# Softmax attention of a four-block kernel: 64-row score pairs, one shared ring of two PSUM banks, and the last power in groups

## The chip, the core and the metric

The kernel runs on one NeuronCore of a Trainium2 chip. Five engines work side by side and wait for each other through semaphores: TensorE (PE, matmul; its weight loads are PEld), VectorE (DVE), ScalarE (ACT), GpSimd (POOL) and SyncE (SP, which issues most DMAs). Matmuls write PSUM, which has eight banks of 512 fp32 columns on 128 partitions. The metric is the device time of one execution in microseconds; lower is better.

## The reference, cut to what matters

The reference is a chain of four blocks on x of shape (2, 1024, 256): a differential softmax attention, a routed block with attention and an FFN, an attention over a memory with an entmax, and an FFN with ternary weights. Each is added to x after a layer norm. Only the first block (and the start of the next stage) is touched:

```
qkv = layernorm(x) @ Wqkv             # q1, k1, q2, k2: 16 heads of 8; v: 16 heads of 16
A1 = causal_softmax_attention(q1, k1, v)      # scores q.k / sqrt(8)
A2 = causal_softmax_attention(q2, k2, v)
diff = A1 - lam * A2
diff = diff / sqrt(mean(diff^2) + 1e-5) * (1 - LAMBDA_INIT)     # per head and token
x = x + layernorm(diff @ Wproj)
```

## The kernel before, in words

`attention_inputs` (0 to 65 us) normalizes x, multiplies by Wqkv and splits each query and key into three bf16 parts (high, middle, low); the parts go to DRAM (`qk_parts`). SyncE loads them back for each head as stacks of rows: six parts of eight dimensions, 48 rows, for each of the two attentions j. The product of a query stack and a key stack gives the score with nearly fp32 precision. In `QS` and `KS` before the change rows 0 to 47 hold the stack, rows 48 to 95 are zero and rows 96 to 98 hold the row maximum in three bf16 parts (`QS`) against a constant near one (`KS`); j is a dimension of the tile. GpSimd fills the constant rows with three memsets (L198, L203, L208), and the load of head 0 (L161) waits for the last.

`attention_heads` runs 16 heads. For each head and each of the four (j, batch) pairs there are two sets of score matmuls:

- the natural set (`unit_scores`, L642): queries on the partitions, keys on the columns, 96 rows of contraction. Units of at most 512 columns, 40 per head, with the causal mask added on the diagonal by a matmul of an identity and a mask (L645). They go to three PSUM banks `nat`; VectorE reduces each to a row maximum (L515). The maxima of a head are joined (L519), turned by TensorE into the bank `misc` (L653), split in three bf16 parts by VectorE from that bank (L530 to L538), and written by six DMAs into rows 96 to 98 of `QS` (L420).
- the transposed set (`scores`, L678): keys on the partitions, queries on the columns, 128 rows of contraction, so that the maximum is subtracted by the matmul itself. A head has nine chunks n with four matmul groups c = (j, batch) each. Each group goes to one of two banks `sc`, and ScalarE takes the exponential (L610). GpSimd zeroes the part above the diagonal of five chunks (L482). Two chunks later TensorE multiplies the four probability tiles by the values (`values`, L698, four matmuls on 32 columns of the array each), accumulating in `OT`.

The order of TensorE is written out by hand in `period` (L717 on): for each chunk n and each c, the scores of c; then the natural units that are due (of the next head and of the one after it, spread evenly over the 36 places); after c = 1 the turned outputs of the last head (in chunks 2 and 3) and the values of chunk n - 2. The outputs of a head are copied from `OT` by ScalarE (L592, at the end of chunk 1), turned in two rounds by TensorE into `misc` (L714), copied again by ScalarE (L599), normalized by VectorE (L544, L546), and combined and squared by GpSimd (L450, L455, L460). GpSimd also runs a slice of the ternary weights of the last block in each head (L340 to L351, after the diagonal of chunk 4), and raises the mean square of the outputs to the power -0.5 for each head (L468, 16 columns). The last head's power (604.42 to 607.35 us) is the last instruction of the stage; `output_and_route` starts after it with VectorE's scaling of the outputs (L937).

## Time and profile before

| | us |
|---|---|
| median of 3 runs (1664.35 to 1668.11) | 1667.57 |
| the profiled execution | 1665.8 |
| its span, first to last instruction | 1664.0 |
| TensorE busy / weight loads | 1490.1 / 1010.6 |
| VectorE busy | 1249.8 |
| ScalarE busy | 1109.4 |
| GpSimd busy | 1080.9 |
| granted TensorE clock, mean over the span | 0.963 |

Busy shares are averages over stages with different limits. The attention heads span 65 to 608 us. In a timeline row the first number is the start in us from the beginning of the span, the second the time to the end of the merged group; `xN` counts the merged instructions (a fp32 matmul is two records), and brackets hold the idle time of the engine before the group and what ended it.

### The profile page before, as it was taken

Reading aid. Unit: us, or ns where it says so; the run is one execution under the profiler, and the core shown is the slowest. Engines: PE = TensorE matmul, PEld = TensorE weight load, DVE = VectorE, ACT = ScalarE, POOL = GpSimd, SP = SyncE. Lnnn points to the kernel's source line nnn. Section 1 sums busy time; section 2 is a strip of 40 time slices with the busy share of each in tenths; the row PEclk is TensorE's granted clock in tenths of the full one; section 3 lists DMA queues with packets and bytes.
Section 4 is the critical chain, followed back from the end, with each engine's and each line's share of the span. In section 5 each row is a group of like instructions: output and inputs, shape, how many; then the busy total and the mean of one; then the engine's idle time right before and its main releaser. Section 6 shows DMA issues by size and latency. Waiting matters only on the chain. (4 is left out here: it accounts for less than half of the span.)

```text
span 1664.0 us, 26578 instructions
## 1 busy us (share of the span) xinstructions
PE 1490.1 (90%) x8478; PEld 1010.6 (61%) x8540; DVE 1249.8 (75%) x3420; ACT 1109.4 (67%) x2385; POOL 1080.9 (65%) x1273
## 2 busy tenths in 40 slices
PE   7899999999999857887848999999999999987998
PEld 4334434434434236766646888878888888776675
DVE  5688788788788229652359999999999999973433
ACT  2146666666666737222237999999999999994332
POOL 6205466566566572142248999999999999973353
PEclk9779999999999979999979999999999999999999
DMA  5301001001000033830000000000000100000000
GB/s 203 114 21 38 23 22 38 22 22 39 21 22 21 2 103 116 320 121 17 35 1 1 1 1 1 1 1 1 1 1 1 51 1 1 1 1 1 1 26 26
DMA packets 39812, 59.84 MB, mean 36 GB/s; under 512 B 9132, under 2 KB 33592, under 8 KB 38776
## 3 DMA queue, kind: packets, MB, share of 16 engines
q1 hardware_dynamic: 39528, 56.03, 10.4%
q10 hardware_dynamic: 144, 2.10, 0.3%
q8 instruction: 69, 1.13, 0.3%
q14 instruction: 71, 0.58, 0.1%
HBM read 40.93 MB, written 16.78 MB: 35 GB/s over the span
## 5 line engine op out<-in xcount | busy, mean ns | idle before, releaser
L610 ACT ACTIVATE a_PT<-a_sc 128x512 f32<-128x512 f32 x576 | 317.7, 600 | 187.8 <-PE a_sc L678 128.7
L515 DVE TENSOR_REDUCE a_mpart<-a_nat 128x1 f32<-128x512 f32 (+3 forms) x640 | 364.1, 627 | 78.5 <-PE a_nat L645 41.4
L2046 DVE BATCH_NORM_STATS2 c_stat<-c_R 128x6 f32<-128x512 f32 x576 | 380.9, 678 | 1.7 <-ACT c_R L1965 1.6
L2010 POOL TENSOR_SCALAR c_R<-big,c_negtau 128x256 f32<-128x256 f32 x264 | 300.6, 1165 | 33.1 <-DVE c_negtau L2079 27.0
L2010 POOL TENSOR_SCALAR c_R<-c_Z,c_negtau 128x256 f32<-128x256 f32 x255 | 290.7, 1164 | 16.0 <-DVE c_negtau L2112 15.2
L642 PE MATMUL a_nat<-mem 96*128 96x512 bf16 (+3 forms) x768 | 242.7, 343 | 22.0 <-DVE a_mpart L515 11.8
L1882 PE MATMUL c_z<-mem,c_R 128*128 128x256 f32 x1024 | 231.5, 379 | 0.0
L482 POOL TENSOR_SCALAR_AFFINE_SELECT a_PT<-a_PT 128x512 f32<-128x512 f32 x128 | 79.0, 636 | 221.9 <-ACT a_PT L610 221.9
L1965 ACT ACTIVATE c_R<-c_Z,c_negtau 128x256 f32<-128x256 f32 x513 | 215.8, 516 | 0.4 <-DVE c_negtau L2112 0.4
L1965 ACT ACTIVATE c_R<-big,c_negtau 128x256 f32<-128x256 f32 x504 | 212.6, 515 | 3.2 <-DVE c_negtau L2079 1.7
L1882 PEld LDWEIGHTS c_z<-mem,c_R 128*128 128x128 f32 x1024 | 192.9, 190 | 25.4
L678 PE MATMUL a_sc<-mem 128*128 128x512 bf16 (+3 forms) x706 | 196.8, 326 | 9.0 <-ACT a_PT L610 6.2
L678 PEld LDWEIGHTS a_sc<-mem 128*128 128x128 bf16 x768 | 61.2, 97 | 179.4 <-ACT a_PT L610 148.4
L698 PE MATMUL a_OT<-a_PT,a_VH 128*32 128x512 f32 (+3 forms) x1536 | 154.6, 498 | 3.3 <-POOL a_PT L482 3.2
L1894 PE MATMUL c_T<-ident,c_R 128*128 128x128 f32 x768 | 106.7, 282 | 35.9 <-ACT c_R L1960 35.3
L1882 PE MATMUL c_z<-mem,c_hT 128*128 128x256 f32 x512 | 119.6, 388 | 8.8 <-ACT c_hT L1989 8.8
L642 PEld LDWEIGHTS a_nat<-mem 96*128 96x128 bf16 x768 | 76.2, 99 | 76.4 <-DVE a_mpart L515 48.3
L1906 PE MATMUL c_y<-mem,c_R 128*128 128x256 f32 x512 | 120.7, 386 | 0.0
L1894 PEld LDWEIGHTS c_T<-ident,c_R 128*128 128x128 f32 x768 | 85.9, 142 | 56.7 <-ACT c_R L1960 46.7
L1960 ACT ACTIVATE c_R<-c_T 128x512 f32<-128x512 f32 x192 | 104.0, 595 | 22.5 <-PE c_T L1894 22.5
L1882 PEld LDWEIGHTS c_z<-mem,c_hT 128*128 128x128 f32 x512 | 98.7, 195 | 24.4 <-ACT c_hT L1989 9.4
L645 PE MATMUL a_nat<-mask,ident_bf 128*128 128x128 bf16 x512 | 106.7, 227 | 0.0
(313 smaller groups left out, 2445.1 us busy)
## 6 DMA issues: line engine op xcount, KB each, us to landing
mem<-qk_parts SPq DMA_DIRECT2D x360, 32.0 KB
qk_parts<-a_parts SPq DMA_DIRECT2D x16, 384.0 KB, 2.6
made<-f_made SPq DMA_DIRECT2D x24, 256.0 KB, 2.8
mem<-made SPq DMA_DIRECT2D x3, 2048.0 KB, 7.7
X<-in_L_attn_x_dram SPq DMA_DIRECT2D x4, 512.0 KB, 6.9
mem<-in_L_ffn_wq_dram SPq DMA_DIRECT2D x1, 2048.0 KB, 13.9
ternary<-f_W_T ACTq DMA_DIRECT2D x1, 2048.0 KB, 8.7
mem<-in_L_ffn_wo_dram SPq DMA_DIRECT2D x1, 2048.0 KB, 14.4
```

The costliest lines, as they stand in the source:

```text
L515: dve.tensor_reduce(mpart[:, b, j:j + cnt, i, k0 // 512], src, AX.X, ALU.max).then_inc(s_max, 1)
L610: act.activation(PT[:, n % 3, c, :], sc[:, u % 2, :], ACT.Exp, scale=SCALE0).then_inc(s_exp, 1)
L642: ins = pe.matmul(out, QS[0:MROW, h.buf, j, q:q + P], KS[0:MROW, h.buf, j, b * T + k0:b * T + k0 + w], start=True, stop=diag >= w)
L645: ins = pe.matmul(out[:, diag:diag + P], K.ident_bf[:], K.mask[:], start=False, stop=True)
L678: ins = pe.matmul(sc[:, u % 2, col:col + w], KS[:, h.buf, j, b * T + kt * P:b * T + (kt + 1) * P], QS[:, h.buf, j, b * T + q0:b * T + q0 + ...
L698: ins = pe.matmul(OT[32 * c:32 * c + 32, q0:q0 + w], VH[:, h.buf, b * TB + kt, :], PT[:, n % 3, c, col:col + w], start=(kt == 0), stop=(kt ...
L1882: ins = pe.matmul(z_ps[:, n % SCORE_BANKS, e * NMEM:(e + 1) * NMEM], L, G[:, m, h, :], start=(m == 0), stop=(m == 1))
L1894: ins = pe.transpose(T_ps[:, n % TURN_BANKS, (2 * e + m) * P:(2 * e + m + 1) * P], whole(i, h)[:, m * P:(m + 1) * P], K.ident[:])
L1906: ins = pe.matmul(y_ps[:, k % 2, 0:D], weights(i, h, m), K.VO[:, m, h, :], start=(n == 0), stop=(n == 15))
L1965: act.activation(split(i, h) if r < NR else whole(i, h), scores_of(i)[:, h, :], ACT.Relu, bias=threshold(i, r, h)).then_inc(s_ra[r], 1)
L2010: pool.tensor_scalar(split(i, h) if r < NR else whole(i, h), scores_of(i)[:, h, :], threshold(i, r, h), 0.0, ALU.add, ALU.max).then_inc(s_ ...
L2046: dve.bn_stats(stat[:, r, b, :], R[:, slot(i), b, :]).then_inc(s_stat, 1)
```

## The change

- `QS` and `KS` lose their dimension j: attention j = 0 has rows 0 to 50, j = 1 rows 64 to 114 (48 of the stack, 3 of the maximum). Both score sets now contract over 48 or 51 rows in one half of the array, and natural units go in pairs (j = 1, j = 0), into four banks. The two zero memsets go; one memset of a tile half as wide stays.
- The mask of 128 rows is added in two steps of 64 rows, on the half that the unit uses; a copy of identity and mask with swapped halves is made by four DMAs.
- The bank `misc` goes. The turned maxima and the two turned outputs take their turn in the two banks of the exponentials, in one written-out order (`IN_TURN`); each waits for whoever read the bank two places before. ScalarE copies the turned maxima to SBUF (`mcopy`), and VectorE splits from there.
- The order in `period`: scores of c = 0 (or 2), the natural pairs that are due (20 pairs over 18 places), scores of c + 1, then as before turned outputs and values. The turn of the maxima has a fixed place, after the first score of chunk 6. The scores of a chunk go in the order j = 0, 1, 0, 1. ScalarE copies a turned output after the exponential of c = 1 instead of after c = 3.
- The power of the last head goes to the next stage, in four groups of four columns; `scaled(g)` waits for its own group. There GpSimd's constants (iota, memsets, selects) move behind the first root and the memory's root.

```
-STK = 6 * HD0
-MROW = 96
+STK, SIDE = 6 * HD0, 64
 def max_units():
+    shapes = [[(i, 0, 512)] for i in range(3, TB)] + [[(7, 512, 512)], [(2, 0, 384)], [(6, 512, 384)],
+                                                      [(1, 0, 256), (5, 512, 256)], [(0, 0, 128), (4, 512, 128)]]
+    return [(j, segs) for segs in shapes for j in (1, 0)]
+SET_ORDER = (0, 2, 1, 3)
+MAX_CHUNK = 6
+def turned_banks():
+    order = [("max", 0)]
+    for h in range(H0):
+        for n in range(len(PROB_CHUNKS)):
+            for c in range(4):
+                order.append(("exp", h, n, c))
+                if n == MAX_CHUNK and c == 0 and h + 1 < H0:
+                    order.append(("max", h + 1))
+                if n in (2, 3) and c == 1 and h > 0:
+                    order.append(("out", h - 1, n - 2))
+    return order + [("out", H0 - 1, r) for r in range(2)]
...
             root(0)
             pool.wait_ge(s_xn, GT)
-            pool.memset(K.QS[:].bitcast(F32), 0.0).then_inc(s_zero, 1)
+            pool.memset(K.KS[:].bitcast(F32), BF16_ONES).then_inc(s_zero, 1)
...
-            pool.memset(K.KS[0:MROW].bitcast(F32), 0.0).then_inc(s_zero, 1)
...
-            pool.memset(K.KS[MROW:P].bitcast(F32), BF16_ONES).then_inc(s_zero, 1)
...
-        nat, sc, OT, misc = ps("nat", [P, 3, 512]), ps("sc", [P, 2, 512]), ps("OT", [P, T]), ps("misc", [P, 512])
+        nat, sc, OT = ps("nat", [P, 4, 512]), ps("sc", [P, 2, 512]), ps("OT", [P, T])
+        bank_of = lambda *what: sc[:, TURN_OF[what] % 2, :]
...
+            def copy_max(h):
+                act.wait_ge(s_mT, h.count(1, 1))
+                if h.n > 0:
+                    act.wait_ge(s_msp, h.count(1))
+                act.activation(mcopy[:], bank_of("max", h.n)[0:32, 0:P], ACT.Copy).then_inc(s_mc, 1)
...
+            def unit_pair(h, u):
...
+                if NU * h.n + u >= 4:
                     pe.wait_ge(s_max, h.count(NU, u - 2))
+                pair = [units[u], units[u + 1]]
+                for n in range(len(pair[0][2])):
+                    for e, (b, j, segs) in enumerate(pair):
+                        (i, k0, w), rows = segs[n], slice(SIDE * j, SIDE * j + STK)
+                        q, out = b * T + i * P, nat[:, (u + e) % 4, n * w:(n + 1) * w]
+                        ins = pe.matmul(out, QS[rows, h.buf, q:q + P], KS[rows, h.buf, b * T + k0:b * T + k0 + w],
+                                        start=True, stop=i * P - k0 >= w)
...
+                    for half, (unit, mask) in enumerate(((K.ident_bf, K.mask), (K.ident_swap, K.mask_swap))):
+                        for e, (b, j, segs) in enumerate(pair):
+                            (i, k0, w), side = segs[n], slice(SIDE * j, SIDE * j + SIDE)
+                            diag = i * P - k0
+                            if diag < w:
+                                out = nat[:, (u + e) % 4, n * w + diag:n * w + diag + P]
+                                ins = pe.matmul(out, unit[side, :], mask[side, :], start=False, stop=half == 1)
...
+            def bank_for(*what):
+                k = TURN_OF[what]
+                if k >= 2:
+                    kind, h, *rest = IN_TURN[k - 2]
+                    if kind == "exp":
+                        pe.wait_ge(s_exp, 4 * NCH * h + 4 * rest[0] + rest[1] + 1)
+                    elif kind == "max":
+                        pe.wait_ge(s_mc, h + 1)
+                    else:
+                        pe.wait_ge(s_ons, 2 * h + rest[0] + 1)
+                return bank_of(*what)
...
-                    for c in range(4):
+                    for c in (0, 2):
                         scores(h, n, c)
-                        k = 4 * n + c
-                        for _ in range(NU * (k + 1) // (4 * NCH) - NU * k // (4 * NCH)):
+                        if n == MAX_CHUNK and c == 0 and h.next(1).exists():
+                            turn_max(h.next(1))
+                        k = 2 * n + c // 2
+                        for _ in range(NU // 2 * (k + 1) // (2 * NCH) - NU // 2 * k // (2 * NCH)):
                             next(between, None)
-                        if c == 1:
+                        scores(h, n, c + 1)
+                        if c == 0:
                             if last.exists() and VLAG <= n < VLAG + 2:
                                 turn_outputs(last, n - VLAG)
...
+            for g in range(NG):
+                last = K.rms[:, rows(g), H0 - 1]
+                pool.tensor_tensor(last, last, K.mhalf[:, 0:GT], ALU.pow).then_inc(s_rms, 1)
             ternary_slice(pool, K, H0 - 1, s_tern, 0)
+            y_root(0)
...
             def scaled(g):
+                dve.wait_ge(s_rms, g + 1)
```

## Rows read from the trace of the kernel before

**Rows 1.** Windows by stage: busy time and instructions per engine, TensorE clock, DMA share, GB/s.
```profile
65.00:98.00 33.00, 30.46 (x104) 9.45 (x105) 31.63 (x61) 0.00 (x0) 1.17 (x2) 0.55 0.16 43
...
128.75:563.18 434.43, 416.71 (x3177) 172.67 (x3231) 349.72 (x699) 302.34 (x561) 265.28 (x433) 1.00 0.10 26
```
**Rows 2.** Timeline of TensorE, one middle head: start, length, instructions (PV, L698).
```profile
284.33 1.07 PE L698 MATMUL a_OT<-a_PT,a_VH 128*32 128x512 f32 x8
287.44 1.07 PE L698 MATMUL a_OT<-a_PT,a_VH 128*32 128x384 f32 x16
...
291.51 1.06 PE L698 MATMUL a_OT<-a_PT,a_VH 128*32 128x512 f32 x8
...
295.15 1.06 PE L698 MATMUL a_OT<-a_PT,a_VH 128*32 128x512 f32 x8
...
301.69 1.07 PE L698 MATMUL a_OT<-a_PT,a_VH 128*32 128x512 f32 x8
...
315.45 1.07 PE L698 MATMUL a_OT<-a_PT,a_VH 128*32 128x512 f32 x8
```
**Rows 3.** Timeline of one slot of the last head, TensorE and ScalarE.
```profile
582.44 1.07 PE L698 MATMUL a_OT<-a_PT,a_VH 128*32 128x256 f32 x16
...
583.44 0.60 PE L678 MATMUL a_sc<-mem 128*128 128x512 bf16 x2
...
583.87 1.08 ACT L610 ACTIVATE a_PT<-a_sc 128x512 f32<-128x512 f32 x2 [0.67 <-PE a_sc L678]
...
584.52 0.88 PE L678 MATMUL a_sc<-mem 128*128 128x512 bf16 x2 [0.47 <-ACT a_PT L610]
...
585.33 1.06 PE L698 MATMUL a_OT<-a_PT,a_VH 128*32 128x512 f32 x8
```
**Rows 4.** Timeline of ScalarE in slot 2 of the middle head.
```profile
289.84 1.03 ACT L592 ACTIVATE a_OTS<-a_OT 128x1024 f32<-128x1024 f32 x1
290.74 1.11 ACT L610 ACTIVATE a_PT<-a_sc 128x512 f32<-128x512 f32 x2
```
**Rows 5.** Timeline of GpSimd: diagonal selects of chunks 4 and 7.
```profile
301.15 1.22 POOL L482 TENSOR_SCALAR_AFFINE_SELECT a_PT<-a_PT 128x512 f32<-128x512 f32 x2 [5.83 <-ACT a_PT L610]
...
313.74 0.64 POOL L482 TENSOR_SCALAR_AFFINE_SELECT a_PT<-a_PT 128x512 f32<-128x512 f32 x1
```
**Rows 6.** Timeline of VectorE and SP after the split, and DMA landing (KB, us).
```profile
305.99 3.99 DVE L515 TENSOR_REDUCE a_mpart<-a_nat 128x1 f32<-128x512 f32 x7
306.09 3.68 SPq L420 DMA_DIRECT2D mem<-a_msplit  x6
...
mem<-a_msplit SPq DMA_DIRECT2D x6, 4.0 KB, 1.7
```
**Rows 7.** Timeline of the routed stage: matmuls of 64 rows on alternating halves.
```profile
729.41 1.14 PE L1547 MATMUL b_s<-b_qkT 64*128 64x256 f32 x8
730.48 0.29 PE L1549 MATMUL b_s<-mask,ident_bf 128*128 128x128 bf16 x2
```
**Rows 8.** Window of the last head.
```profile
555.00:590.00 35.00, 26.54 (x179) 7.48 (x180) 1.51 (x5) 26.20 (x50) 23.91 (x39) 1.00 0.01 1
```
**Rows 9.** Timeline of the inputs: GpSimd's third memset, SP's issues, VectorE's last part.
```profile
40.56 5.21 POOL L208 MEMSET mem<- 32x6144 f32 x1 [1.48 <-DVE a_xn L230]
...
45.88 8.11 SPq L114 DMA_DIRECT2D mem<-qk_parts  x24
54.03 7.34 SPq L156 DMA_DIRECT2D qk_parts<-a_parts  x8
...
57.73 0.69 DVE L242 TENSOR_TENSOR a_parts<-a_rest,a_parts 128x512 bf16<-128x512 f32 x1 [0.51 <-POOL a_parts L194]
```
**Rows 10.** Timeline of GpSimd at the end of the heads and in the next stage.
```profile
604.42 2.93 POOL L468 TENSOR_TENSOR rms<-rms,mhalf 128x16 f32<-128x16 f32 x1 [0.75 <-DVE rms L554]
...
621.20 0.24 POOL L892 TENSOR_SCALAR f_yr<-f_ymv 128x4 f32<-128x4 f32 x1 [2.02 <-DVE f_ymv L946]
621.51 1.05 POOL L894 TENSOR_TENSOR f_yr<-f_yr,mhalf 128x4 f32<-128x4 f32 x1
```

More of the change, by code:

```diff
@@ L136, in attention_inputs @@
         (s_w, s_lam, s_ident, s_pool, s_pad, s_zero, s_st, s_mv, s_var, s_rstd, s_dve, s_xn, s_turned, s_xT, s_qk, s_v, s_hi, s_rest,
-         s_mid, s_lo, s_vc, s_lame) = (sem(n) for n in "w lam ident pool pad zero st mv var rstd dve xn turned xT qk v hi rest "
-                                       "mid lo vc lame".split())
+         s_mid, s_lo, s_vc, s_lame, s_swap) = (sem(n) for n in "w lam ident pool pad zero st mv var rstd dve xn turned xT qk v hi rest "
+                                       "mid lo vc lame swap".split())
         block = ctx.enter_context(nc.Block())
@@ L152, in _ @@
             load_ffn(sp, K, K.w_ffn)
+            sp.wait_ge(s_ident, 3)
+            for whole, swapped in ((K.ident_bf, K.ident_swap), (K.mask, K.mask_swap)):
+                for half in range(2):
+                    sp.dma_start(swapped[SIDE * half:SIDE * half + SIDE, :],
+                                 whole[SIDE * (1 - half):SIDE * (2 - half), :]).then_inc(s_swap, 16)
             for g in range(NG):
@@ L359, in attention_heads @@
     qk_parts, VA = K.qk_parts, K.VA
-    units = [(b, n) + u for b in range(2) for n, u in enumerate(max_units())]
+    units = [(b,) + u for b in range(2) for u in max_units()]
     NU, NCH = len(units), len(PROB_CHUNKS)
@@ L616, in period @@
                             copy_sums(last)
-                        if VLAG <= n < VLAG + 2:
-                            copy_turned(last, n - VLAG)
+            copy_max(Head(0, 0))
             heads(act, period)
@@ L659, in maxima @@
                     return
-                for u in range(FIRST, NU):
-                    unit_scores(first, u)
+                for u in range(FIRST, NU, 2):
+                    unit_pair(first, u)
                     yield
-                for u in range(FIRST):
-                    if u == GAP or not second.exists():
-                        turn_max(first)
-                        if not second.exists():
-                            return
-                    unit_scores(second, u)
-                    yield
+                if second.exists():
+                    for u in range(0, FIRST, 2):
+                        unit_pair(second, u)
+                        yield
             def scores(h, n, c):
                 u = 4 * n + c
-                j, b = c // 2, c % 2
-                if not isinstance(h.n, int) or 4 * NCH * h.n + u > 1:
-                    pe.wait_ge(s_exp, h.count(4 * NCH, u - 1))
-                col = 0
+                j, b = SET_ORDER[c] // 2, SET_ORDER[c] % 2
+                rows = slice(SIDE * j, SIDE * j + STK + 3)
+                bank, col = bank_for("exp", h.n, n, c), 0
                 for kt, q0, w in PROB_CHUNKS[n]:
-                    ins = pe.matmul(sc[:, u % 2, col:col + w], KS[:, h.buf, j, b * T + kt * P:b * T + (kt + 1) * P],
-                                    QS[:, h.buf, j, b * T + q0:b * T + q0 + w], start=True, stop=True)
+                    ins = pe.matmul(bank[:, col:col + w], KS[rows, h.buf, b * T + kt * P:b * T + (kt + 1) * P],
+                                    QS[rows, h.buf, b * T + q0:b * T + q0 + w], start=True, stop=True)
                     col += w
@@ L736, in period @@
                     pass
-            for u in range(FIRST):
-                unit_scores(Head(0, 0), u)
-            for _ in maxima(Head(0, -1)):
-                pass
+            for u in range(0, FIRST, 2):
+                unit_pair(Head(0, 0), u)
+            for k, _ in enumerate(maxima(Head(0, -1))):
+                if k == (NU - FIRST + GAP) // 2 - 1:
+                    turn_max(Head(0, 0))
             heads(pe, period)
```

101 lines of the change are left out of this document (42 added, 59 removed).

## The prediction, made before the change was run

> **What bounds the kernel now.** The windows by stage come first: the sixteen heads of the first attention (65 to 608 us) are a third of the span, and TensorE reads 96% busy through them [rows 1]. That looks like a TensorE bound. The timeline says otherwise. The starts of the probability-value products ("PV", L698), one per chunk, mark slots; nine slots are a head, 284.33 to 315.45, so 31.1 us [rows 2]; heads 1 to 14 together take 434.43, 31.0 each [rows 1]. Now the last head, which has no score sets for maxima ("natural" units) left to do. Its slot is still 585.33 - 582.44 = 2.89 us [rows 3], and it is a chain of latencies, not of work: PV 1.00, its next score matmul to its exponential 0.43 (583.44 to 583.87), two exponentials to the release of a bank and the last score before the next PV, 1.46. An undisturbed slot of a middle head is 3.11 (287.44 - 284.33) [rows 2]: the natural matmul between the second score and PV adds its 0.22, plus a mask. So most of the natural matmuls' time is hidden already, and halving them cannot return 7 us per head.
>
> **The change, part by part, for a middle head.** I count from one PV start (0). Score c=2 starts at 1.00, its exponential at 1.43, the next at 1.91 (two take 1.08, the latency of one being 0.60) [rows 3]; score c=0 of the next slot waits for the first, 2.07; c=1 for the second, 2.56; PV at 2.89.
>
> *Pairs in halves.* Natural matmuls leave the place before PV and stand between scores c=0/c=1 and c=2/c=3. The gaps are 0.49 and 0.55 us. Does a pair fit? In the routed stage 64-row matmuls on alternating halves are in the trace: eight records, four fp32 products of 256 columns, 1024 cycles each, 4096 cycles or 1.71 us in a row; the masks after them start at 730.48, 1.07 us after the first [rows 7]. The halves overlap; about 0.2 of the 1.07 is entry and exit. So a 512-column pair beside a score takes one extra 0.22, masks (four of 128 columns instead of two) 0.11 to 0.22, and it fits: slot 2.9 instead of 3.1. Bounds: full cover 2.89; nothing gained by masks, 3.05.
> The Trainium skill, TensorEngine Tiling (Array Packing), Key Properties, says that changing the tiling mode drains TensorE; the 0.2 us above agrees. By rows I charge 0.1 for each extra switch, around the two turns of outputs. (By the page alone that term would only be unknown, not absent.)
>
> *Turned outputs in the exponentials' ring.* Slot 2 today is 4.07 (287.44 to 291.51) [rows 2]: the ScalarE copy of the sums starts at 2.40 and holds the first exponential to 3.30 (289.84, 290.74) [rows 4]; the turn needs only the copy. New: the turn takes a bank and waits for that first exponential, 3.30 + 0.65 = 3.95, then 0.58 of turning: PV at 4.53, with the switch 4.55. Slot 3: turn after exponential 0, 3.8 against 3.64. The copies of turned outputs fall in the PV hole, free.
>
> *Turned maxima.* They too take a ring place: score c=1 of slot 6 waits for its own slot's exponential: 3.13 instead of 2.56, slot 3.46 where an undisturbed one today is 3.1. The small ScalarE copy sits in the same hole. What follows: VectorE's split, six DMAs (3.68 issuing, 1.7 to landing) [rows 6] and the wait at the next head. The split ends about 4.7 after PV of slot 5 (VectorE does two reductions first), the rows land near 10.1; the next head's first score is at 11.6. No wait, about 1.5 us spare (0 to 2). SP's 24 loads for a later head go out first and are 8 us long at a head's start, as for head 0 (45.88 to 54.0) [rows 9].
>
> *Four natural banks against VectorE.* Seven reductions take 3.99, so 0.57 each, 1.15 a pair [rows 6]; VectorE is 80% busy [rows 1], so it does not bound on average. But the schedule emits twenty pairs over eighteen gaps, and in slot 4's first gap two: the second waits for the pair emitted 1.0 us earlier. That one is ready at 1.7 and reduced at 2.95; score c=1 goes at 3.4 instead of 2.56. Slot 4: 3.7, so slots 4 and 5 together 6.6, against 6.54 (295.15 to 301.69) [rows 2]. (Bounds for slot 4: 2.9 and 3.9.) After the split slot 7 loses about 0.3.
>
> *GpSimd, next in line.* From the diagonal selects of chunk 4 (301.15) through one ternary slice and the outputs to the end of select 7 (313.74 + 0.64) is 13.2 us [rows 5]; PV of slot 0 waits for that. Nothing of it changes. The selects start 0.33 before PV of slot 5, so PV of slot 5 to PV of slot 0 cannot be under 12.9; today it is 13.76 (301.69 to 315.45) [rows 2]. TensorE's own way is 3.46 + 3 x 2.89 + 0.3 to 0.8 = 12.4 to 12.9. I take 13.0.
>
> Head: 2.9 + 4.55 + 3.8 + 3.7 + 2.9 + 13.0 = 30.85, against 31.1: -0.25. Bounds: every gap covered and no GpSimd limit 2.89 x 6 + 4.5 + 3.7 + 3.46 = 29.0; the upper ends 31.9.
>
> **Sum.**
> Inputs: two of three 5.2 us memsets go. SP waited for the last (40.56 to 45.8) before loading head 0, and its last parts left at 54.03 + 7.34 = 61.4. VectorE's last part is ready at 57.73 + 0.69 = 58.4, and one issue is about 0.9; new end 59.4: -2.0 [rows 9]. Four swap copies use SP while it waits: 0 (up to +0.5).
> Start of heads: VectorE paces it (31.6 busy of 33) [rows 1]; one bank more lets TensorE leave earlier, -0.6 (0 to -1.2). Head 0, no outputs or slices: nine slots at about -0.22, -2.0 (0 to -3).
> Heads 1 to 13: 13 x -0.25 = -3.3. Head 14 has no second set, today 434.43 - 13 x 31.12 = 29.9; new 30.85, +0.9. Head 15: slots 2 and 3 alone, +0.6.
> End: the second turn no longer waits for the first copy, -0.7. Power: the 16-column one (2.93) stood between stages; the first group of four costs 1.05 (as L894), TensorE waits for that only: 2.93 - 1.05 = -1.9 [rows 10]. The other three run beside VectorE's scaling; ternary slice and y root come 4.2 later in the stage, of which the root waited 2.0 for its input [rows 10], and the fill of constants (about 1.3) moves behind it: within 0.9.
> Total -2.0 - 0.6 - 2.0 - 3.3 + 0.9 + 0.6 - 0.7 - 1.9 = -9.0. The profiled execution took 1665.8 (span 1664.0 and 1.8 around it): 1656.8; it lies 1.8 under the median of the runs, so 1658 in that frame.
>
> **Rivals.**
> *A, the chain is looser than I count* (GpSimd and VectorE catch up, the double pair hides). For it: the slack of 0.5 in each gap. Against: slots 2 and 3 are long today with and without natural units. Head 29.0 to 30.2: -2.0 x 13 and -0.9 for head 14 and the rest give 1632 at the full end. Chance 0.17.
> *B, TensorE's work is the bound after all*, as its 96% suggest. Scores and natural sets are 36 x 0.22 us each per head, so half of both is 7.9; VectorE's 25 us (349.72 / 14) then bounds, -6 a head: about 1570. The last head's 2.89 speaks against it. Chance 0.03. The same page, Theoretical Speedup, gives up to 2x for contractions of 64 or less; by that rule alone this would be the result.
> *C, bank waits cost a little more*: masks at 0.055 each in five gaps and 0.3 more at the double pair; head 31.5, 13 x 0.4 = +5.2, head 14 +1.5, the rest -6: 1668. Chance 0.19.
> *D, slower: the granted clock.* Natural units alone ran at a mean of 0.55 in the first stretch [rows 1]; the last head kept 1.00 with TensorE 76% busy [rows 8]. With half the rows quiet TensorE could fall to 1.2 GHz between 130 and 560. At that level PV and two scores on the chain, 1.44, double; with a third of the slots low this is 9 x 0.48 = 4.3 a head, +60: 1720. It decides once more than a twentieth of the slots are low. Chance 0.07.
> *E, the halves do not overlap for bf16 into separate banks.* A pair then needs 0.66 to 0.88 in a gap of 0.49 to 0.55, about 0.3 a gap; outside the GpSimd stretch that is 2.5 a head, +35: 1693. Rows 7 speak against it. Chance 0.04.
>
> **Numbers.** Forecast 0.50, A 0.17, B 0.03, C 0.19, D 0.07, E 0.04. Range: 1640 to 1672 leaves out B, D, E and the far half of A on one side. The likeliest case alone holds 1651 to 1664. A measurement of this kernel can tell about 0.2% (3.3 us) from none. Faster: A, B and nine tenths of the forecast, 0.66; same: the rest of the forecast and half of C, 0.14; slower: half of C, D, E, 0.20.
>
> **What would show it.** Slots of the new profile: 2.9 undisturbed, 4.5 and 3.8 where outputs turn, about 3.5 with turned maxima, 3.7 in slot 4 behind two pairs. ScalarE idle of about 0.5 before c=2. Select of chunk 7 ending right before PV of slot 0. Granted clock 1.00 from 105 to 590. Heads starting near 63, VectorE's first scaling about 1.9 earlier after the outputs. Wrong would be a head under 30 (then the ring or GpSimd does not bind) or over 31.5, or a score waiting for the rows of the maxima.

## The result, and the profile after

The changed kernel takes 1674.87 us (median of 6 runs, 1671.64 to 1680.71); the kernel before, run beside it, 1667.24 (1663.92 to 1669.40). The ratio is 1.0053, 95% interval 1.0038 to 1.0067: slower by about half a per cent, where 1658 was forecast. The profiled execution is the slowest of the six (1680.71, span 1679.0), so the sums over its trace below come out larger than the difference of the medians. Medians and ranges are over all executions of a kernel, but ratios leave out an execution more than 1.5% above the kernel's fastest, which concerns scores48 alone (two of its four).

The loss shows first in one column of one view, the granted clock. Windows of TensorE in the changed kernel: busy time and instructions, granted clock (1.00 is 2.4 GHz, 0.50 is 1.2), DMA share, GB/s.
```profile
100.00:110.00 10.00, 9.70 (x49) 0.50 0.04 13
110.00:120.00 10.00, 8.85 (x94) 0.83 0.01 2
200.00:260.00 60.00, 49.65 (x520) 1.00 0.09 26
260.00:270.00 10.00, 8.82 (x62) 0.66 0.06 15
570.00:580.00 10.00, 7.74 (x42) 0.50 0.00 0
```
Before, the clock was 1.00 in all of heads 1 to 14 [rows 1] and in the last head [rows 8]. Now it comes up late at the start of head 0, dips in some of the middle heads, and has a mean of 0.55 from the first to the last slot of the last head (569.29 to 604.80).

The schedule itself came out as forecast. The starts of the probability-value products (PV) of head 1, all at clock 1.00, answer to [rows 2]. Timeline of TensorE:
```profile
128.27 1.06 PE L741 MATMUL a_OT<-a_PT,a_VH 128*32 128x512 f32 x8
131.15 1.07 PE L741 MATMUL a_OT<-a_PT,a_VH 128*32 128x384 f32 x16
...
135.21 0.63 PE L753 MATMUL a_sc<-ident,a_OTS 128*128 128x128 f32 x4 [1.11 <-ACT a_PT L635]
...
135.77 1.06 PE L741 MATMUL a_OT<-a_PT,a_VH 128*32 128x512 f32 x8
139.57 1.06 PE L741 MATMUL a_OT<-a_PT,a_VH 128*32 128x512 f32 x8
143.22 1.07 PE L741 MATMUL a_OT<-a_PT,a_VH 128*32 128x384 f32 x16
146.11 1.06 PE L741 MATMUL a_OT<-a_PT,a_VH 128*32 128x512 f32 x8
...
159.24 1.06 PE L741 MATMUL a_OT<-a_PT,a_VH 128*32 128x512 f32 x8
```
The differences, with the three starts that are left out here (149.63, 152.64, 155.52), are 2.88, 4.62, 3.80, 3.65, 2.89, 3.52, 3.01, 2.88, 3.72: the forecast had 2.9, 4.55, 3.8, 3.7, 2.9 and 13.0 for the last four (13.13 here). The head is 30.97, forecast 30.85. The wait of 1.11 ahead of the turned outputs is the ring's: TensorE stands until the exponential has left the bank.

In the last head the same work takes longer. Timeline of TensorE in the changed kernel, PV of slots 0, 6, 7 and 8, slot 7 to be read against [rows 3]:
```profile
569.29 1.93 PE L741 MATMUL a_OT<-a_PT,a_VH 128*32 128x512 f32 x8
...
596.44 1.93 PE L741 MATMUL a_OT<-a_PT,a_VH 128*32 128x256 f32 x16
...
599.60 1.09 PE L721 MATMUL a_sc<-mem 51*128 51x512 bf16 x2 [0.68 <-ACT a_PT L635]
600.62 1.93 PE L741 MATMUL a_OT<-a_PT,a_VH 128*32 128x512 f32 x8
604.80 1.93 PE L741 MATMUL a_OT<-a_PT,a_VH 128*32 128x512 f32 x8
```
and PV of slots 0 and 8 in the kernel before:
```profile
563.18 1.07 PE L698 MATMUL a_OT<-a_PT,a_VH 128*32 128x512 f32 x8 [0.66 <-POOL a_PT L482]
...
588.22 1.06 PE L698 MATMUL a_OT<-a_PT,a_VH 128*32 128x512 f32 x8
```
PV is 1.93 long instead of 1.06, and the slot 600.62 - 596.44 = 4.18 instead of 2.89. There is no more work in it than before; it is the latency chain at half the clock. From PV of slot 0 to PV of slot 8 the last head takes 35.5 us (569.29 to 604.80) instead of 25.0 (563.18 to 588.22).

Start and tail, in the order first exponential, copy of the last sums, power by groups, scaling. Timeline of ScalarE, GpSimd and VectorE in the changed kernel:
```profile
95.27 0.60 ACT L635 ACTIVATE a_PT<-a_sc 128x512 f32<-128x512 f32 x1 [9.10 <-PE a_sc L721]
610.87 1.02 ACT L611 ACTIVATE a_OTS<-a_OT 128x1024 f32<-128x1024 f32 x1 [2.48 <-PE a_OT L741]
619.03 2.01 POOL L950 TENSOR_TENSOR rms<-rms,mhalf 128x4 f32<-128x4 f32 x2 [0.98 <-POOLq L379]
620.08 0.76 DVE L985 TENSOR_TENSOR f_dn<-DIFF,rms 128x256 f32<-128x256 f32 x2 [1.37 <-POOL rms L950]
```
and of the kernel before (its power is in [rows 10]):
```profile
98.81 0.60 ACT L610 ACTIVATE a_PT<-a_sc 128x512 f32<-128x512 f32 x1 [39.52 <-remote]
595.51 1.02 ACT L592 ACTIVATE a_OTS<-a_OT 128x1024 f32<-128x1024 f32 x1 [4.78 <-PE a_OT L698]
607.72 2.77 DVE L937 TENSOR_TENSOR f_dn<-DIFF,rms 128x256 f32<-128x256 f32 x8 [3.37 <-PEq L364]
```

From these the balance of the profiled executions up to the scaling (620.08 against 607.72, +12.36): at the first exponential the changed kernel is 3.5 ahead; at slot 0 of head 1 only 0.5 (128.27 against 128.75), so head 0 gave back 3.0 while the clock stayed low; heads 1 to 14 take 569.29 - 128.27 = 441.0 against 434.4 (+6.6), where fourteen undisturbed heads would be 433.6; the last head from PV of slot 0 to PV of slot 8 takes 35.5 against 25.0 (+10.5); from there to the copy of the sums 6.1 against 7.3 (-1.2), and from the copy to the scaling 9.2 against 12.2 (-3.0). The head 0 of this execution is an unlucky one: in three kernels below with the same start (last_full, last_half, moved) the clock came up earlier, and from the first exponential to slot 0 of head 1 they took 30.0, 31.5 and 31.2 where this execution took 33.0 and the kernel before 29.9. The remaining 2.6 of the span fall in later stages, which the change doesn't touch except for GpSimd's order, and are within what two single executions of this kernel differ by.

### The profile page after: what moved, and what is told of

It is laid out like the page before. It is cut to its first block and busy times, and to the rows that moved or that the text cites. A ratio compares the mean times of both kernels' runs of the same rounds, so it can differ in the third digit from the quotient of the medians.

```text
span 1679.0 us, 27707 instructions
## 1 busy us (share of the span) xinstructions
PE 1441.4 (86%) x9052; PEld 982.3 (59%) x9052; DVE 1249.7 (74%) x3420; ACT 1120.9 (67%) x2401; POOL 1070.8 (64%) x1274
## 5 line engine op out<-in xcount | busy, mean ns | idle before, releaser
L721 PE MATMUL a_sc<-mem 51*128 51x512 bf16 (+3 forms) x768 | 217.1, 349 | 53.8 <-ACT a_PT L635 51.7
L500 POOL TENSOR_SCALAR_AFFINE_SELECT a_PT<-a_PT 128x512 f32<-128x512 f32 x128 | 78.6, 638 | 242.1 <-ACT a_PT L635 241.9
L670 PE MATMUL a_nat<-mem 48*128 48x512 bf16 (+3 forms) x768 | 181.3, 353 | 23.6 <-DVE a_mpart L534 20.7
L721 PEld LDWEIGHTS a_sc<-mem 51*128 51x128 bf16 x768 | 55.2, 95 | 222.7 <-ACT a_PT L635 163.6
L741 PE MATMUL a_OT<-a_PT,a_VH 128*32 128x512 f32 (+3 forms) x1536 | 168.4, 536 | 2.9 <-POOL a_PT L500 1.7
L1954 PEld LDWEIGHTS c_y<-mem,c_R 128*128 128x128 f32 x512 | 98.4, 198 | 12.8
L1972 PE MATMUL c_T<-mem,ident 128*128 128x256 f32 x368 | 86.9, 379 | 0.0
```

The costliest lines, as they stand in the source:

```text
L670: ins = pe.matmul(out, QS[rows, h.buf, q:q + P], KS[rows, h.buf, b * T + k0:b * T + k0 + w], start=True, stop=i * P - k0 >= w)
L721: ins = pe.matmul(bank[:, col:col + w], KS[rows, h.buf, b * T + kt * P:b * T + (kt + 1) * P], QS[rows, h.buf, b * T + q0:b * T + q0 + w], ...
L741: ins = pe.matmul(OT[32 * c:32 * c + 32, q0:q0 + w], VH[:, h.buf, b * TB + kt, :], PT[:, n % 3, c, col:col + w], start=(kt == 0), stop=(kt ...
L1954: ins = pe.matmul(y_ps[:, k % 2, 0:D], weights(i, h, m), K.VO[:, m, h, :], start=(n == 0), stop=(n == 15))
```

## The experiments

The theory that was tested, **R (rows)**: a product that contracts over 48 or 51 rows leaves most of TensorE's array idle, and for this the chip grants the low clock, whatever the busy column says. The rivals: **I (idle stretches)**, the clock falls because the ring's waits leave TensorE idle; **S (schedule)**, the last head and the double pair are slow in themselves. Each kernel was timed against the kernel before on the same chip; ratios are to it, and where a kernel is set against the changed one, its 1.0053 is the other term.

### Rows in the kernel before: nat48 and short

nat48:
```
- QS[0:MROW, ...], KS[0:MROW, ...]   # natural products, 96 rows
+ QS[0:STK, ...],  KS[0:STK, ...]    # 48 rows
```


> The kernel before, its natural score products alone contracting over rows 0:48 instead of 0:96 (rows 48 to 95 were zero, so nothing is left out). Theory R (rows): TensorE's granted clock falls because instructions that contract over few rows leave most of the array idle. The last head has no natural products, so its first eight slots stay at 25.0 us and clock 1.00; the middle heads may show a first dip or none: 1667 to 1672 us. Theory I (idle gaps): the clock falls because the changed kernel's waits on the two-bank ring leave TensorE idle longer at a stretch; here no wait changes, so 1667 within 1 us and no dip. Both allow no change; a dip would speak for R alone.

short, with the line above and:
```
- MROW = 96
+ MROW = STK
- matmul(sc..., KS[:, ...], QS[:, ...])                      # turned score products, 128 rows
+ matmul(sc..., KS[0:STK + 3, ...], QS[0:STK + 3, ...])      # 51 rows
```
(GpSimd's second memset also fills rows 0 to 95 of `KS` with the constant now, since the maxima stand in rows 48 to 50.)


> The kernel before with every score product over few rows: maxima in rows 48:51, natural products over 48 rows instead of 96, turned score products over 51 instead of 128; banks, order, waits and all else as before. Theory R: the last head falls to the low clock and its slots 0 to 8 take about 31 us instead of 25.0, the middle heads show a few dips of 2 to 3 us, the start of head 0 comes up about 3 us later: +10 to +17 us, 1677 to 1684 us. Theory I (idle gaps from the ring): nothing changes, 1667 within 1 us, granted clock 1.00 in all of the last head.

Measured: nat48 1773.07 (1771.34 to 1779.95), ratio 1.0650 (1.0629 to 1.0671). short 2024.85 (2015.88 to 2035.94), ratio 1.2163 (1.2128 to 1.2198). Both theories missed nat48 by a hundred microseconds, and no theory foresaw the size of short. There are two different costs. Window of TensorE in nat48:
```profile
120.00:550.00 430.00, 421.72 (x2562) 0.98 0.08 22
```
and in short:
```profile
120.00:550.00 430.00, 429.76 (x1805) 0.57 0.06 15
```
In its middle heads nat48 is slow at full clock, so that loss is not the clock's. Timeline of TensorE in nat48, the rhythm of turned and natural products (weight loads left out):
```profile
320.15 0.39 PE L678 MATMUL a_sc<-mem 128*128 128x512 bf16 x1
...
320.48 0.39 PE L642 MATMUL a_nat<-mem 48*128 48x512 bf16 x1
...
320.79 0.39 PE L678 MATMUL a_sc<-mem 128*128 128x256 bf16 x2
```
and in the kernel before:
```profile
296.15 0.39 PE L678 MATMUL a_sc<-mem 128*128 128x512 bf16 x1
...
296.38 0.38 PE L642 MATMUL a_nat<-mem 96*128 96x512 bf16 x1
```
Before, the next product starts 0.23 us after the last (296.15, 296.38). Each change between a 48-row and a full product makes that 0.31 to 0.33: about 0.1 per change. A head of nat48 is 37.7 (PV starts 301.06 to 338.79) against 31.1; at 0.1 each that would be some 65 changes a head that nothing hides, an estimate. Over heads 1 to 14 of the profiled execution this comes to 89.2 (523.6 against 434.4). Another 26.3 lie ahead of head 1, and there the clock has its part: it stays at 0.50 from 70 to 140 us, where the kernel before has 1.00 from about 102 on, though nothing but the rows of the natural products differs. The last head, which has no natural products, takes the same 25.0 as before, at 1.00. The busy column gives no warning: the stalls count as busy (421.72 of 430).

short has fewer such changes than nat48 (its turned and natural products are of one mode and follow each other at 0.23 us), and yet the clock is 0.57 as a mean over heads in which TensorE reads 99.9% busy. No wait, bank or order was changed against the kernel before. That is theory R, and waits on a ring (theory I) cannot explain it, for there is no ring. Stalls at changes of rows hide in the busy column too, but nat48 has more of them and kept 1.00 from 150 us on.

### The last head: last_full and last_half
```
+ if not h.next(1).exists():
+     pe.wait_ge(s_max, NU * H0)
+     for _ in range(2):
+         pe.matmul(nat[:, k % 4, :], K.ident_bf[0:P, :], KS[0:P, h.buf, 0:512], start=True, stop=True)
```
at each of the last head's eighteen places; last_half has `0:STK` in place of `0:P`. The results are not used.

> The changed kernel with two idle products of 128x128 by 512 columns over all 128 rows (results unused) at each of the 18 places of the last head where the other heads have a pair of natural products. Theory R: the last head returns to clock 1.00 and slots of about 2.9 us, so slots 0 to 8 take about 25.5 instead of 31.3 us: -5 to -7 us against the changed kernel, 1668 to 1670 us (ratio to before 1.000 to 1.002). Theory I: the gaps are filled, so the same -5 to -7. Theory S (the last head is slow for the ring's own order, not for the clock): the added products only cost, 1675 or more.

> The same kernel as last_full, but the idle products contract over 48 rows only: the same number of instructions, columns and busy time. Theory R: the clock stays at the low level in the last head, slots 0 to 8 take 31 us or more: 1675 to 1677 us. Theory I (busy time or gaps decide, not rows): as last_full, 1668 to 1670 us. Theory S: 1675 or more.

Measured: last_full 1671.31 (1665.99 to 1674.80), ratio 1.0028 (1.0016 to 1.0039); last_half 1674.37 (1671.96 to 1680.34), ratio 1.0053 (1.0034 to 1.0072). Full rows gave back 0.0025 of 1666, 4.2 us where 5 to 7 were expected, half rows nothing. (The expectations count 31 us for slots 0 to 8 of the last head of the changed kernel; that is one slot short, and against the 25.0 of the kernel before stand 35.5.) Windows of TensorE in last_full:
```profile
560.00:570.00 10.00, 8.21 (x37) 0.58 0.01 2
570.00:580.00 10.00, 8.59 (x54) 0.91 0.01 2
```
and in last_half:
```profile
560.00:570.00 10.00, 8.54 (x36) 0.50 0.01 2
570.00:580.00 10.00, 9.11 (x45) 0.50 0.00 0
580.00:590.00 10.00, 9.03 (x65) 0.88 0.01 2
```
In these two executions the clock was already down when head 15 began (568.25 and 569.28): the last natural product of head 14 starts at 553.1 and 553.4, and PV takes 1.9 from 562.99 and 560.48 on. With full rows the clock is up again some 10 us earlier. This speaks for R over I, but weakly: last_half also came back in the end, and slots 0 to 8 took 30.1 in last_full and 30.2 in last_half, since the full-row products cost time of their own (slots of 3.25 at clock 1.00 where last_half has 2.88). S is out, since with 2.88 a slot at clock 1.00 is as short as before.

### The double pair: moved
```
- for _ in range(NU // 2 * (k + 1) // (2 * NCH) - NU // 2 * k // (2 * NCH)):   # two pairs at k = 8 and 17
+ for _ in range(1 + (k in (9, 17))):
```
(The expectation's "place 9 of 18" is k = 9, the second gap of slot 4.)

> The changed kernel with its double pair of natural products moved from after score product 8.0 to after 8.2's neighbour (place 9 of 18, the second of slot 4) and nothing else changed. The forecast's step for slot 4 (3.7, two pairs against VectorE's four maxima): there the double pair stands ahead of the pair of exponentials that the next product waits for; after the move slot 4 should take 3.1 to 3.3 us instead of 3.65, 13 or 14 times: -5 to -7 us, about 1668 to 1670. If slot 4 is bound elsewhere (VectorE's backlog moves along), slot 5 takes what slot 4 gives and the time stays at 1675. Theory R says nothing of it: the dips and the last head stay.

Measured: 1675.09 (1672.70 to 1676.80), ratio 1.0054 (1.0041 to 1.0067), the changed kernel's own. Timeline of TensorE in a head of moved, PV of slots 3 to 6 (that of slot 7 starts at 213.92):
```profile
200.83 1.07 PE L741 MATMUL a_OT<-a_PT,a_VH 128*32 128x512 f32 x8
203.71 1.07 PE L741 MATMUL a_OT<-a_PT,a_VH 128*32 128x384 f32 x16
207.11 1.07 PE L741 MATMUL a_OT<-a_PT,a_VH 128*32 128x512 f32 x8
210.78 1.07 PE L741 MATMUL a_OT<-a_PT,a_VH 128*32 128x256 f32 x16
```
Slot 4 fell to 2.88, and slots 5 and 6 took 3.40 and 3.67 for it: the 13.09 from PV 3 to PV 7 were 13.07. The expected second outcome: VectorE's backlog moved along, and from PV 5 to the next head's PV 0 it is 13.1 in the changed kernel and 13.2 in moved, the GpSimd limit of the forecast: PV of slot 0 waits for GpSimd's select (L500) in the head shown above.

### Filling the waits: warm, warm_all, warm_half, warm_one, warm_last
```
+ def fill_next(h, pairs, n):        # ahead of turn_outputs: n = 4 in slot 2, 1 in slot 3; heads 0 to 13 only
+     unit = NU * (h.n + 1) + FIRST + 2 * pairs
+     pe.wait_ge(s_max, unit - 2)
+     fill(nat[:, unit % 4, :], h.next(1).buf, n)    # the product of last_full, n times
...
+ elif h.n >= H0 - 2:                # a place with no pair left
+     pe.wait_ge(s_max, NU * H0 - 2)
+     fill(nat[:, 0, :], h.buf, 2)
...
+ fill(OT[:, 0:512], 0, 1)           # after each pair ahead of head 0
```
warm has all three over 128 rows; warm_all adds one more product at the end of every slot but slot 3; warm_half is warm with 48 rows (64 to 111) in each of these products; warm_one has none ahead of head 0 and one instead of two in the empty places; warm_last is warm_one without `fill_next`.

> The changed kernel with idle full-row products (128 rows, 512 columns, results unused) where TensorE otherwise waits: one after each pair ahead of head 0, four ahead of the turned outputs of slot 2, one ahead of those of slot 3, two at each place of heads 14 and 15 that has no pair. Theory R: the clock rises as early as in the kernel before (about 101 us), no dips in heads 1 to 13, and at most one short stretch of low clock in the last head: -10 to -15 us against the changed kernel, 1660 to 1665, the sum that the forecast made at full clock. If the dips come from something else (an event that lies outside the chain), the middle heads keep them and only the start and the last head gain: 1667 to 1670.

> As warm, and one more idle full-row product at the end of each slot but slot 3, where TensorE waits 0.34 to 0.47 us for the exponentials. Theory R: the dips are gone even where warm keeps one; the added product costs nothing where it fits (0.22 us in a gap of 0.34) and up to 0.1 us a slot where it does not: 1658 to 1672. If warm already has no dip, this is equal or up to 10 us worse.

> The kernel warm with every idle product contracting over 48 rows (64 to 111) instead of 128: the same instructions, columns and places. Theory R: the rows are what keeps the clock up, so most of warm's gain over the changed kernel is gone: dips in the middle heads, a low last head, 1671 to 1677. Theory I (idle stretches bring the clock down, whatever fills them): as warm, 1661 to 1665.

> The kernel warm with no idle products ahead of head 0 (in warm the first exponential came 0.8 us later for them) and one instead of two at each place of heads 14 and 15 without a pair (in warm nine slots of the last heads took 3.25 us instead of 2.88). If the clock stays: -0.4 to -1 us at the start, -2.5 to -3 at the end, 1659 to 1660, a version faster than both kernels. If one product in a place is too few: the last head falls to the low clock, 1664 to 1668.

> The kernel warm_one without the idle products ahead of the turned outputs: only heads 14 and 15 have any. Theory R: the last head stays up, the middle heads show their two to four dips of 2 to 3 us again: warm_one + 4 to + 9 us, 1664 to 1668.

| kernel | median (range) us | ratio to before (95%) |
|---|---|---|
| warm | 1662.67 (1661.55 to 1667.84) | 0.9988 (0.9980 to 0.9997) |
| warm_all | 1672.46 (1670.71 to 1677.59) | 1.0049 (1.0034 to 1.0063) |
| warm_half | 1659.69 (1657.55 to 1662.18) | 0.9968 (0.9956 to 0.9979) |
| warm_one | 1659.54 (1658.16 to 1663.87) | 0.9970 (0.9959 to 0.9982) |
| warm_last | 1666.28 (1664.18 to 1670.66) | 1.0002 (0.9993 to 1.0011) |

The work of the kernel is unchanged in all five; only products nobody uses were added, and three of them beat the kernel before, warm by as little as a measurement can tell. Window of TensorE over the middle heads in warm_one:
```profile
120.00:550.00 430.00, 371.00 (x3763) 1.00 0.09 26
```
warm_half has 370.04 busy and 1.00 there, the changed kernel 356.41 and 0.98, warm_last 357.41 and 0.97. The idle products ahead of head 0 did not help: in warm they had the clock at 0.84 over 70 to 80, but it was at 0.50 again from 100 until about 109.

warm_last less warm_one prices the dips of the middle heads at 6.7 us by the medians (1666.28, 1659.54), 5.3 by the ratios; the changed kernel less warm_last prices the last two heads at 8.5 (1.0053, 1.0002 of 1666). warm_all kept the clock and lost for its cost: nine slots of a head take 3.25, 4.62, 3.80, 3.64, 2.89, 3.53, 3.32, 2.88 and 3.82, together 31.75 instead of 30.97, since the product at a slot's end stands in the way of the next slot's turned products in three places.

warm_half is the miss of theory R as it was put: 48-row products cured the dips as well as full ones, and they cost less. From PV of slot 0 to PV of slot 8 its last head takes 26.1 at clock 1.00, that of warm 28.9, with slots of 2.89 and 3.25. So R alone is not the whole: few rows and idle time add up, and either is a lever. Rows did it without idle in short; idle products of few rows undid it in warm_half.

### The ring, the tail: ring and tail

ring is the kernel before with the change's `bank_for`, `copy_max` and `turned_banks`; `misc` is gone, three natural banks and all rows stay:
```
- nat, sc, OT, misc = ps("nat", [P, 3, 512]), ps("sc", [P, 2, 512]), ps("OT", [P, T]), ps("misc", [P, 512])
+ nat, sc, OT = ps("nat", [P, 3, 512]), ps("sc", [P, 2, 512]), ps("OT", [P, T])
...
- pe.transpose(misc[:, k * P:(k + 1) * P], OTS...)
+ pe.transpose(bank[:, k * P:(k + 1) * P], OTS...)     # bank = bank_for("out", h.n, r)
```


> The kernel before with the bank ring alone: turned maxima and turned outputs go through the two banks of the exponentials (as in the changed kernel, with the copy of the maxima on ScalarE), everything else as before, all contractions over 96 and 128 rows. The forecast's steps: slot 2 takes about 1.3 us more, slot 3 0.7 more, slot 6 0.3 more, with VectorE's work as before: +1 to +2 us a head, 1680 to 1700. Theory R: the clock stays at 1.00 in every head, since no product lost rows. Theory I: the waits on the ring bring dips and a low last head here too.

Measured: 1683.37 (1682.35 to 1685.83), ratio 1.0112 (1.0099 to 1.0125). Timeline of TensorE in a head of ring:
```profile
325.86 1.07 PE L737 MATMUL a_OT<-a_PT,a_VH 128*32 128x384 f32 x16
329.93 0.63 PE L749 MATMUL a_sc<-ident,a_OTS 128*128 128x128 f32 x4 [0.66 <-ACT a_PT L640]
330.48 1.07 PE L737 MATMUL a_OT<-a_PT,a_VH 128*32 128x512 f32 x8
```
Slot 2 is 4.62 against 4.07 (+0.55, forecast +0.48), slot 3 3.80 against 3.64, slot 6 344.57 - 340.82 = 3.75 against 3.16; the head 32.24 against 31.12, +1.1. The expectation's sizes were too large for slots 2 and 3 and too small for slot 6; its range for the whole held. The clock was 1.00 over 120 to 550: in the middle heads, where natural products fill the gaps, the ring's waits do not bring it down when the products have their rows. In the last head they do, once. Window, and timeline of TensorE in slot 2 of the last head of ring:
```profile
550.00:600.00 50.00, 41.51 (x292) 0.97 0.01 1
586.12 1.05 PE L749 MATMUL a_sc<-ident,a_OTS 128*128 128x128 f32 x4 [1.10 <-ACT a_PT L640]
587.11 1.94 PE L737 MATMUL a_OT<-a_PT,a_VH 128*32 128x512 f32 x8
```
TensorE waits 1.10 for the ring (it is busy 0.79 of the 2 us from 584 to 586), the clock reads 0.54 over 586 to 588, and PV takes 1.94; by 590 it is at 1.00 again. Slots 2 and 3 are 5.06 and 4.89 instead of the ring's 4.62 and 3.80. Theory R had expected 1.00 in every head, so this one dip is theory I's: idle time alone can bring the clock down, with full rows and no natural products. So the halves give 32.24 - 30.97 = 1.27 a head and the ring takes 1.12.

tail is the kernel before with the power by groups and GpSimd's new order alone:
```
- rms(Head(0, H0 - 1))
...
+ for g in range(NG):
+     last = K.rms[:, rows(g), H0 - 1]
+     pool.tensor_tensor(last, last, K.mhalf[:, 0:GT], ALU.pow).then_inc(s_rms, 1)
```


> The kernel before with the tail alone changed: the last head's root-mean-square power in four groups of four at the start of the next stage, and the first y root and the memory's roots moved up in GpSimd's order. The forecast's step: from the copy of the last sums to the scaling -2.6 us, of which -1.9 reach the end: ratio 0.9985 to 0.9995. A rival: the next stage is bound by its loads or by the ternary slice, and the time stays at 1.000.

Measured: 1664.44 (1661.38 to 1666.53), ratio 0.9994 (0.9985 to 1.0002): -1.0 us, between nothing and the 1.9 that were forecast, and not told apart from nothing by its interval. With the copy of the sums at the same 595.51 as before, the scaling starts at 604.80 instead of 607.72, so 2.9 are won there; by the medians not all of it reaches the end.

### What the fourth bank is for: noring, noring_warm; and scores48

Still open was whether the dips need the ring's idle time at all. noring is the changed kernel with a bank of its own for turned maxima and outputs, and three natural banks:
```
- nat, sc, OT = ps("nat", [P, 4, 512]), ps("sc", [P, 2, 512]), ps("OT", [P, T])
+ nat, sc, OT, misc = ps("nat", [P, 3, 512]), ps("sc", [P, 2, 512]), ps("OT", [P, T]), ps("misc", [P, 512])
...
- pe.wait_ge(s_max, h.count(NU, u - 2))
+ pe.wait_ge(s_max, h.count(NU, u - 1))
```
noring_warm adds to it the idle products of warm_one, with three instead of four in slot 2. scores48 is the kernel before with `KS[0:STK, ...]`, `QS[0:STK, ...]` in the turned score products alone.

> The changed kernel without the ring: turned maxima and outputs in a bank of their own again, three natural banks instead of four, natural pairs in halves of the rows and everything else as changed. At full clock a head should lose what the kernel ring showed it to cost where GpSimd does not bound: slot 2 4.62 to about 4.07, slot 3 3.80 to 3.64, so about 30.2 instead of 30.97, -9 to -11 us. If the few rows bring the dips by themselves, they stay, and so does the low last head: 1664 to 1667. If the dips need the ring's idle 1.1 us, the middle heads stay at 1.00 and only start and last head are low: 1657 to 1661.

> The kernel noring with idle full-row products as in warm_one (three ahead of the first turned outputs, one ahead of the second, one at each empty place of heads 14 and 15). If both effects add up: warm_one's 1659.5 less 9 to 11: 1649 to 1652. If the added products no longer fit in the shorter wait of slot 2, up to 0.3 us a head comes back: 1654.

> The kernel before with its turned score products alone contracting over 48 rows instead of 128; the rows of the maxima are left out of them, so the exponentials are not shifted. Natural products stay at 96 rows. Switches between 48-row and full products then stand around every natural product, as in nat48: +6 us a head, about 1770 at full clock. If few rows in the scores bring the clock down, the last head (no natural products) runs at the low level, slots of about 4.2, and the middle heads partly: 1790 to 2000. If only rows and number of switches together did it in short, the last head stays at 1.00 and the time at 1770.

Measured: noring 1702.90 (1698.05 to 1706.94), ratio 1.0223 (1.0204 to 1.0242); noring_warm 1718.74 (1710.06 to 1729.76), ratio 1.0322 (1.0289 to 1.0355); scores48 1749.24 (1733.81 to 1782.74), ratio 1.0423 (1.0404 to 1.0442), of 1733.81 and 1738.13 alone. The first two are plain misses; the third is below both of its ranges too, though its sign in the last head came. Timeline of TensorE in noring:
```profile
301.25 1.07 PE L724 MATMUL a_OT<-a_PT,a_VH 128*32 128x512 f32 x8
303.52 0.34 PE L659 MATMUL a_nat<-mem 48*128 48x384 bf16 x2 [0.61 <-DVE a_mpart L532]
305.39 1.07 PE L724 MATMUL a_OT<-a_PT,a_VH 128*32 128x512 f32 x8
```
A pair needs two banks at once; with three it waits for VectorE to have reduced the pair ahead of it, and with it wait the turned products behind it: this slot is 4.14 where the changed kernel has 3.7. The fourth bank, and so the ring, is what makes the pairs pay; as a test of idle against rows noring is spoilt, since it has idle of its own. It dips in the middle heads like the changed kernel (0.95 over 120 to 550); no more can be said.

scores48 isolates the rows in the last head. Windows of TensorE, one in head 14 and two in its last head (630.23 to 662.26):
```profile
610.00:620.00 10.00, 9.98 (x76) 1.00 0.01 2
630.00:640.00 10.00, 8.93 (x46) 0.57 0.00 0
650.00:660.00 10.00, 9.47 (x41) 0.50 0.00 0
```
As long as 96-row natural products stand between the short ones the clock is 1.00. The last of them starts at 617.9, and the clock falls in the first slot of the last head; it is back at 1.00 over 642 to 648 and low again after. That head takes 32.0 from PV of slot 0 to PV of slot 8. The kernel before has the same last head with full rows, stays at 1.00 [rows 8] and takes 25.0. Banks, waits and order are the same in both, so here few rows alone bring the clock down.

## Why the prediction was wrong

The step that failed is the granted clock, in the forecast's words "Granted clock 1.00 from 105 to 590". Every term of its sum for the heads was worked out at full clock; the runs show a low clock in head 0, in dips of the middle heads and through most of head 15, and that is where the time went. The rest of the working can be held against the runs one by one:

- **Slots of a middle head**: right to 0.15 each, head 30.97 for 30.85. The ring's price is seen alone in ring (+0.55, +0.16, +0.6 in slots 2, 3, 6), the double pair's backlog in moved, the GpSimd limit in both. The gain of 0.25 a head was 0.15.
- **Inputs and start**: -3.5 at the first exponential for -2.6; a little more than forecast. But "head 0 ... -2.0" became +3.0, because the natural pairs ahead of it, of 48 rows now, did not bring the clock up by 101 us as before; it stood at 0.50 until about 113. (Before it came up at about 102. nat48, with 48 rows in the natural products alone, stood at 0.50 until 140.) In the other kernels with this start head 0 lost between nothing and 4.2.
- **Heads 1 to 14**: forecast -3.3 + 0.9 = -2.4, in the profiled execution +6.6. Fourteen undisturbed heads would have given -0.8; the rest are dips, 5.3 to 6.7 us by warm_last against warm_one.
- **Head 15**: forecast +0.6, measured +10.5 from PV of slot 0 to PV of slot 8: four slots of 4.18 (for 2.89 where nothing is turned), and 6.16 and 5.56 where the outputs turn. Up to the copy of the sums 1.2 come back, since before the last PV waited 2.5 for GpSimd's select and now 0.92.
- **End and power**: from the copy of the sums to the scaling 9.2 instead of 12.2, so -3.0 for -2.6. By tail about 1.0 of the power's 1.9 reaches the end, within 0 and 2.5 by its interval.

Together these give -3.5 + 3.0 + 6.6 + 9.3 - 3.0 = +12.4 up to the scaling. (The forecast's own sum, 1656.8 and 1.8, is 1658.6; it wrote 1658.)

With the waits filled (warm_one) the time is 6.0 us under that of before by the medians (1659.54, 1665.52), 5.0 by the ratio, where the forecast's sum had -9.0. In its profiled execution two places fall short of the sum. Head 0 took 34.1 for 29.9 before: warm_one's clock over 90 to 120 us is 0.55, and no kernel with 48-row products ahead of head 0 had it up to stay as early as the 96-row products did (last_full came nearest, at about 104 for 102). And the last head had one more stretch at the low clock and took 29.5 for 25.0.

Rival D named the mechanism, "with half the rows quiet TensorE could fall to 1.2 GHz", and gave it 0.07. It had the price of a low slot about right (1.44, measured 4.18 - 2.89 = 1.29) and its place wrong: it looked to the middle heads, where only dips came, and took the last head's "1.00 with TensorE 76% busy" [rows 8] for a reserve. That row was of 128-row products. It did name the other hint, the first stretch with natural products alone at a mean of 0.55 [rows 1], but those were of 96 rows, and it set the 1.00 of the last head against them. The share of busy time that the profile prints is blind to rows: 96.6% busy at clock 1.00 before, 83% at 0.98 after, 99.9% at 0.57 in short.

The Trainium skill bears on this in three places. "TensorE: Matmul & The Clock Gate", A second HAM failure mode: psum-queue depth-cycling, says that cycling through PSUM banks with short idles between groups of products makes the clock swing between its levels. By that rule ring should have shown it and the changed kernel owed its loss to the ring; the runs bear it out in one place only: ring kept 1.00 over 120 to 550 and dipped once in its last head, behind the wait of 1.10. The same page of the Trainium skill, What's actually happening, has the clock follow how busy TensorE has been; short, 99.9% busy by the profile's count and low, shows that rows enter as well. The Trainium skill, "TensorEngine Tiling (Array Packing)", Key Properties, has the drain at a change of mode; nat48 puts 0.1 us on it, the figure that the prediction had taken from [rows 7].

Open: how rows and idle time weigh against each other, since noring failed as a test of it, ring shows idle alone in one dip of one execution, and half-row products did nothing measurable in last_half and everything in warm_half; why the dips fall in some heads and not in others (their places differ from execution to execution); and where the rest of the tail's gain goes.

## What to carry to other kernels

Cutting a product's contraction rows is not free even where nothing else changes: ask of each stretch what TensorE still does afterwards, and look at the granted clock there first, the last, thinnest stretch of a loop above all. Where a chain of latencies bounds and TensorE has idle gaps, unused products in the gaps are cheap and can be worth more than the change itself (here 14 us, 1.0053 less 0.9970), but only where the gap is; one in the wrong place costs its length in every slot. And a product of few rows between full ones costs about 0.1 us each way. Putting such products side by side saves that, but a stretch that holds nothing else is what brought the clock down (short).

## What was not expected of the hardware

- Natural products over 48 instead of 96 rows, alone among full ones, cost 106.7 us (nat48). Most of it came at full clock, where a product started 0.31 to 0.33 us after the last instead of 0.23; the rest came at the start, where the clock stood at 0.50 until 140 us.
- With every score product short, the clock had a mean of 0.57 over 120 to 550 us while TensorE read 99.9% busy (short), and the kernel took 2024.85 us for 1666.4.
- Idle products of 48 rows held the clock in the heads as well as those of 128 (warm_half, warm), and cheaper: 1659.69 and 1662.67.
- A turned and a natural product on different halves of the rows start together, 0.01 apart, and the next product follows at 0.22 as if there had been one. Timeline of TensorE in the changed kernel:
```profile
289.30 0.39 PE L721 MATMUL a_sc<-mem 51*128 51x512 bf16 x1
289.31 0.60 PE L670 MATMUL a_nat<-mem 48*128 48x512 bf16 x2
289.53 0.38 PE L721 MATMUL a_sc<-mem 51*128 51x512 bf16 x1
```
